# Sixteen-head attentions with the values as stationary blocks: three layers of a twelve-layer kernel rewritten, with new merge lists

## The chip, the cores and the metric

The kernel runs on one core of a Trainium2 chip. The metric is device microseconds of one execution. An execution is one program per engine: TensorE (PE; its weight loads are shown apart as PEld), VectorE (DVE), ScalarE (ACT), GpSimd (POOL), and SyncE (SP), which issues the DMAs. The engines run their own instructions in order and wait for each other on semaphores.

## The reference, cut to what matters

The model is a chain of twelve residual layers over `x` of 64 sequences x 64 tokens x 128 channels, with a context of 128 tokens a sequence. Three of the layers hold a self-attention with 16 heads of 8 channels over the 64 tokens of a sequence; they are what the change touches:

```python
# L1_attn ("lin" in the kernel): linear attention, causal
q, k = relu(q), relu(k)
kv = cumsum(k[..., :, None] * v[..., None, :], axis=2)
num = einsum('bhnd,bhnde->bhne', q, kv)
den = einsum('bhnd,bhnd->bhn', q, cumsum(k, axis=2))[..., None] + 1e-5
y = (num / den) @ wo
# L1_ffn ("m1"): causal softmax attention with rotary positions, then a mixture of experts
attn = softmax(where(causal, q @ k.T / sqrt(8), -inf)); out = (attn @ v) @ wo
# L2_attn ("loc"): softmax attention over the 64 tokens, with biases
o = (softmax(q @ k.T / sqrt(8)) @ v) @ w_out + b_out
```

The other nine are two wide cross-attentions (the costliest layers), a recurrence, a layer of small experts, a single-head cross-attention, a state-space layer, two further mixtures and a sum. They are not changed.

## The kernel before, in words

The 64 sequences are worked off in 4 passes of 2 slots with 8 sequences each. Slot 0 and slot 1 hold independent data (buffers `_0` and `_1`, half of PSUM each, as four banks of 512 float32 columns). Each engine's program for a slot is a generator that stops (`yield`) before each wait. `weave` (L105) merges the two slots' programs on each engine by a list of bits in `ORDER` (L76): the list says, step by step, which slot goes on. So the order on each engine is fixed when the kernel is built, and one slot's work is to fill the other's waits.

All matmuls of the layers concerned are float32. The trace shows each of them as two matmul records (a transpose as one), and the order of the program, quoted below, as one.

A 16-head attention of one slot runs over 4 tiles (`TILES`) of 128 tokens, that is 2 sequences each, after the projections (L617 makes the values, ACT writes them to `Vbd` at L1180):

- the scores of a tile: L800 for "lin", L650 (with the causal mask at L645) for "m1" and "loc";
- DVE masks them (L1655, "lin") or subtracts the maximum (L1627, L1628), and ACT takes the exponential (L1195);
- for softmax, the probabilities are transposed on PE (L677) and copied back by ACT (L1202). "lin" has its scores with the keys on the partitions already;
- `head_outputs` (L628) multiplies them with the values. A block of probabilities, 128 rows (two heads x 64 keys) by 64 queries, is the stationary operand; the values of the two heads, 16 columns, and two columns of ones that give the sums of the probabilities, stream through it: 16 matmuls of 18 columns a tile. The result has the queries on the partitions;
- DVE's `head_out` divides: reciprocal of 16 sums a token (L1614 or L1616; for "lin" an addition of 1e-5 at L1613 first), then a product of 128 columns into `kvT` (L1617).

After the fourth tile `project` transposes the result (four transposes, L471 into bank 1), ACT copies it back to `kvT` (L1115, in "loc" with the bias of the values), and four matmuls with the output weights follow (L486, `ps<-wts,kvT`). There are 3 layers x 4 passes x 2 slots = 24 such attentions, 96 tiles.

PE may start the second half of the transposes of tile t+1 only when `head_out` of tile t is done, since they share a bank; the same holds for the scores of tile t+2 in "lin".

At the program's start the weights that follow a normalisation are centred by one matmul a chunk (L693) with a copy by ACT (L1237), before the first pass goes on.

Of the kernel before, what the change touches and what calls it, by code (L numbers as in the profile page):

```python
# [13 lines left out]
D = 128  # L14
BATCH, SEQ, CTX = 64, 64, 128
SLOTS = 2
GB = 8
# [38 lines left out]
CONSTS = [("ident", 128), ("center", 128), ("hmask8", 8), ("cos", SEQ), ("sin", SEQ),  # L56
          ("causal_add", SEQ), ("causal_T", SEQ), ("upto", 128), ("iota", 16)]


def offsets(table):  # L60
    at, out = 0, {}
    for name, n in table:
# [10 lines left out]
C_AT, C_N = offsets(CONSTS)  # L73


ORDER = dict(  # L76
    pe=(2498, int(""
        "444822181410880258c01020810000335b7b7fb76bb60450b74eddace45a55a981c92142240a7cdd464838a13656dea0b3e9"
        "e32874c2d73bb00200c3ee57fcddffda6c08001268c63565a0105190872de9abc288201348746cb5f6dfebbb0ddc4f3db7fe"
        "ccd9e70cf2bbfffbfaa87448128a095ef7aa13121a19ed291411ded71eaa4d06b72a42000c5edabfcdbeeaefc1446869d553"  # L80
        "948693bfffc288424a0e4805061000d21b9f9db6f5bdbfedc3fae25fe6df4f5cbcc2556baa8351414884057d866e482c288a"
        "cf6b4a37bddf7a377f14856cea20080f17ea7e2ded944a0e00cc745b8884324eddffce42d04622000080026badf7eeeb75f4"
        "85a5b1dde9ffdee5f1e3dad7eff38b448248a058fa73ca13121c38edb4839f4ffffffd67ef77ddffbfff2a38d2db79531010"
        "15fd17f99eaa89608ea7dff", 16)),
    act=(1741, int(""
        "888040194410648209080404e67ff6f67bbef2ab0492a31941100e002110a576bda6f5c23a11356d5141fab51ffffa80826a"
        "8caaee1010b344a904a00b6e14cfbdf67fffbfed30f173477ffe928f0221182100a972fe2903fe58ac4a0b722548fb2d37ff"
        "bb860e7bbe2944555f1901e9c0080840d25793f7dffcbfffefbebb20692a561b012016002084466eedd5f75b6e4b5a0db54a"
        "698f930ffa871a52765b1088acd5b8fe400000201cf6e77becffefbff8cdb35c9d7dd15809026021009a776ce857dffeff7f"
        "79f7b7dbef0c78df748c95e097de0871ff", 16)),  # L90
    dve=(2030, int(""
        "10019c448c84102064c044501430ad2f6ecce5e711071e9739cba21341769d70d150b9b21d1c1e314e2edafd8332312308e7"
        "3466dfaecbbddecf14ca128e5ac0294e48802480148cb6ae89820a5edb6f1f4cfd94675f18f967fff8f03d7e1c3996e71f32"
        "0b8918eb4630d7e30ea3181192b62ccfebb36e6cb77ffdd60d98e25c9022acc6484a45220000086cdddddddccfa5efe4e5f0"
        "f3ac6254b8176f26c4950b89c3d1a0f1453b8ddbd99d672f86641d4fb46e6798b7545f7d87131b30988a175cd5404a204008"
        "183012eddcd9978c8f6a6bff3e78d3b5fd78f137594c655dc2f320b8a196b6b11edefffdf2ffcd7bfff7f1e31c596dbf000e"
        "b27dfd", 16)),
    pool=(610, int(""
        "84c56482d685653532821a33934b77e63fb25c04a2531b1afc0ff65229612d4362fbbb1f8db49519a8887db362b52a42162b"
        "936abfef29e2d841784938a97a33fa9512c28e49fffeb67fd1d", 16)),  # L100
    sp=(26, int(""
        "e0e573", 16)))


def weave(program, order):  # L105
# [5 lines left out]
    for k in range(count - 1, -1, -1):  # L111
# [12 lines left out]
TURNS = ["lat", "rnn", "lora", "lora.c", "x1", "lin", "lin.y", "m1", "m1.y", "rms", "x2.c0", "x2.c1", "x2",  # L124
         "loc", "loc.y", "m2", "m2.oh", "m2.x", "ctx0", "ctx1", "x3", "ssm", "m3", "m3.oh"]
# [30 lines left out]
def build(nc, x, ctxin, ctok_in, fold, cols, weights, consts, out):  # L156
# [4 lines left out]
    with stack:  # L161
# [7 lines left out]
        cst = sb("cst", C_N)  # L169
# [16 lines left out]
        def C(name):  # L186
            at, n = C_AT[name]
            return cst[:, at:at + n]
# [194 lines left out]
        def pair_at(t, bb, j):  # L383
            return 1024 * (t % 2) + 512 * (j // 4) + 256 * bb + 64 * (j % 4)
# [7 lines left out]
        with nc.Block() as block:  # L392
# [71 lines left out]
            def _(pe):  # L464
# [1694 lines left out]
```

## Time and profile before

| | us |
|---|---|
| median of 3 runs (2421.55 to 2429.14) | 2424.98 |
| the profiled execution | 2427.39 |
| its span, first to last instruction | 2425.6 |

TensorE has 2312.0 us of busy time, 95% of the span; VectorE 61%, ScalarE 48%, GpSimd 38%. The mean granted TensorE clock is 0.991 of full speed. The DMA engines are almost idle after the start. A busy PE is not PE at its peak: the end of each matmul is modelled, with the time in which its last results drain.

### The profile page before, as it was taken

To read this page: it belongs to the slowest core of one execution; us is meant where nothing else is said; L and a number is where in the kernel's file an instruction comes from. 1 tells how busy PE (TensorE), PEld (TensorE's weight loads), DVE (VectorE), ACT (ScalarE), POOL (GpSimd) and SP (SyncE) were. 2 spreads that over 40 slices of the span, in tenths; PEclk is the share of its full clock that TensorE was granted. 3 is DMA by queue.
4 is the path that set the end of the run, shared out by engine and by line. 5 is a ranking of instruction groups with operands and counts; after the bars stand their busy time and mean duration, and the time that the engine had idled before them with its cause. 6 is when DMAs were issued, how large, how long until landed. Compare 5 with 4: busy or idle time off the path is not lost.

```text
span 2425.6 us, 41921 instructions
## 1 busy us (share of the span) xinstructions
PE 2312.0 (95%) x16426; PEld 1567.8 (65%) x16426; DVE 1490.3 (61%) x4040; ACT 1163.5 (48%) x2998; POOL 916.8 (38%) x853
## 2 busy tenths in 40 slices
PE   9999989999989999999999999999999999999998
PEld 6766656666766665666666675666666666666665
DVE  6457566666575567666564567756665555665653
ACT  5544334555445533445644453545555445354543
POOL 5334353433234336434332444543323243544310
PEclk9999999999999999999999999999999999999999
DMA  5000000000000000000000000000000000000000
GB/s 235 1 1 1 1 14 1 10 1 27 1 1 1 1 1 10 18 10 1 19 1 1 1 1 5 10 14 10 10 5 1 1 1 1 1 1 1 2 1 14
DMA packets 6821, 26.57 MB, mean 11 GB/s; under 512 B 864, under 2 KB 992, under 8 KB 5984
## 3 DMA queue, kind: packets, MB, share of 16 engines
q1 hardware_dynamic: 6624, 23.89, 2.7%
q8 instruction: 130, 2.13, 0.4%
q14 instruction: 67, 0.55, 0.1%
HBM read 21.79 MB, written 2.10 MB: 10 GB/s over the span
## 4 chain that ended last, share of the span: by engine, by line
PE 75%; DVE 16%; issue 3%; ACT 3%; POOL 3%; DMA 0%; POOLq 0%; DVEq 0%; SPq 0%
PE ps L486 9%; PE ps L499 8%; PE ps L549 7%; PE ps L518 6%; PE ps L510 4%; PE ps L889 4%; PE ps L628 4%; PE ps L603 3%; PE ps L471 3%; PE ps L596 3%; PE ps L650 3%; PE ps L601 3%; PE ps L677 2%; PE ps L846 2%; DVE P L1405 2%
## 5 line engine op out<-in xcount | busy, mean ns | idle before, releaser
L1919 POOL TENSOR_TENSOR P<-P,small 128x384 f32<-128x384 f32 x384 | 316.1, 845 | 564.0 <-DVE small L1430 564.0
L1140 ACT ACTIVATE P<-ps,small 128x192 f32<-128x192 f32 x768 | 315.0, 425 | 134.3 <-DVE small L1422 132.8
L1892 POOL TENSOR_TENSOR small<-small,mhalf 128x4 f32<-128x4 f32 x112 | 126.5, 1130 | 511.9 <-DVE small L1410 255.2
L499 PE MATMUL ps<-kvT,big 128*128 128x192 f32 x1536 | 311.4, 333 | 4.5 <-DVE big L1439 1.8
L499 PEld LDWEIGHTS ps<-kvT,big 128*128 128x128 f32 x1536 | 248.8, 190 | 74.9 <-issue 45.1
L1422 DVE TENSOR_REDUCE small<-ps 128x2 f32<-128x384 f32 x384 | 208.3, 550 | 108.8 <-PE ps L499 100.4
L486 PEld LDWEIGHTS ps<-wts,P 128*128 128x128 f32 x1920 | 232.3, 192 | 45.3 <-issue 30.6
L486 PE MATMUL ps<-wts,P 128*128 128x128 f32 x1920 | 247.8, 278 | 3.8 <-DVE P L1827 2.1
L2009 POOL TENSOR_TENSOR P<-T 128x512 f32<-128x512 f32 x96 | 125.4, 1306 | 197.2 <-DVE T L1709 128.2
L518 PEld LDWEIGHTS ps<-value,big 128*128 128x128 f32 x1536 | 178.6, 192 | 28.3 <-issue 18.6
L518 PE MATMUL ps<-value,big 128*128 128x128 f32 x1536 | 188.0, 278 | 0.1
L549 PE MATMUL ps<-kvT,score 128*128 128x512 f32 x384 | 179.0, 608 | 2.6 <-ACT kvT L1115 2.2
L510 PE MATMUL ps<-cst,P 128*128 128x128 f32 x1152 | 164.8, 275 | 9.0 <-POOL P L1919 3.6
L1140 ACT ACTIVATION_READ_ACCUMULATOR P<-ps,small 128x1 f32 x768 | 160.2, 209 | 0.0
L510 PEld LDWEIGHTS ps<-cst,P 128*128 128x128 f32 x1152 | 131.9, 141 | 32.8 <-issue 12.1
L1315 ACT ACTIVATE P<-ps,col 128x512 f32<-128x512 f32 x128 | 83.3, 685 | 106.8 <-PE ps L893 106.7
L628 PEld LDWEIGHTS ps<-Vbd,P 128*64 128x64 f32 x3072 | 98.8, 138 | 48.2 <-issue 23.9
L549 PEld LDWEIGHTS ps<-kvT,score 128*128 128x128 f32 x384 | 69.7, 192 | 79.5 <-issue 72.5
L1488 DVE SCALAR_TENSOR_TENSOR X<-ps,small,X 128x128 f32<-128x128 f32 x256 | 71.9, 343 | 78.7 <-PE ps L486 75.2
L372 POOL TENSOR_TENSOR big<-big,cst 128x1024 f32<-128x1024 f32 x48 | 103.2, 2155 | 42.7 <-ACT big L1307 23.0
L1627 DVE TENSOR_REDUCE small<-ps 128x8 f32<-128x512 f32 x128 | 87.6, 684 | 50.8 <-PE ps L650 46.9
L1157 ACT ACTIVATE big<-ps 128x512 f32<-128x512 f32 x96 | 57.5, 598 | 122.5 <-PE ps L510 122.4
(287 smaller groups left out, 4495.6 us busy)
## 6 DMA issues: line engine op xcount, KB each, us to landing
ctok<-ctok_dram SPq DMA_DIRECT2D x8, 512.0 KB, 4.1
ctxT<-ctx_dram SPq DMA_DIRECT2D x8, 512.0 KB, 4.1
wts<-weights_dram SPq DMA_DIRECT2D x1, 2530.0 KB, 23.3
wts<-weights_dram SPq DMA_DIRECT2D x1, 2189.0 KB, 17.8
X<-x_dram SPq DMA_DIRECT2D x8, 256.0 KB, 3.5
big<-fold_dram SPq DMA_DIRECT2D x2, 1024.0 KB, 8.5
out_dram<-X SPq DMA_DIRECT2D x8, 256.0 KB, 2.3
wts<-weights_dram SPq DMA_DIRECT2D x1, 1536.0 KB, 25.8
```

The source lines that it names most:

```text
L372: return engine.tensor_tensor(big[s][:, 1024 * (t % 2):1024 * (t % 2) + 1024].rearrange("p (b j t) -> p b j t", b=2, t=SEQ), src[:, 128 * ...
L486: m = pe.matmul(part(s, k, t), tile_of(src, t), w, start=first and t == 0 and c == 0, stop=last and t == TILES - 1 and c == len(pairs) - 1)
L499: m = pe.matmul(ps[s][:, at:at + KEYS], big[s][:, BANK * b + 128 * p:BANK * b + 128 * p + 128], kvT[s][:, keys_at(b):keys_at(b) + KEYS], s ...
L510: m = pe.transpose(part(s, k, p), probs(s, j)[:, PAIR * p + at:PAIR * p + at + 128], C("ident"))
L518: m = pe.matmul(part(s, 1, t), big[s][:, 1024 * t + 128 * k:1024 * t + 128 * k + 128], value[:, at:at + 128], start=(t == 0 and k == 0), s ...
L549: m = pe.matmul(bank(s, qp_bank(g, r) + k), score[:, 128 * block_of(h, nh):128 * block_of(h, nh) + 128], latents(s), start=True, stop=True)
L628: m = pe.matmul(ps[s][64 * bb:64 * bb + 64, at:at + 18], src(bb, j), Vbd[s][:, 18 * (8 * b + j):18 * (8 * b + j) + 18], start=True, stop=True)
L1140: m = act.activation(probs(s, b // 2)[:, to:to + KEYS], ps[s][:, at:at + KEYS], ACT.Exp, bias=small[s][:, 4 * e + p:4 * e + p + 1], accum_ ...
L1422: dve.tensor_reduce(small[s][:, at:at + 2], ps[s][:, BANK * k:BANK * k + 2 * KEYS].rearrange("p (c k) -> p c k", k=KEYS), AX.X, ALU.max, n ...
L1892: pool.tensor_tensor(rstd(s, name, n), variance(s, name, n), mhalf[:, 0:n], ALU.pow).then_inc(*sig("rstd", s))
L1919: m = pool.tensor_tensor(view, view, over(small[s][:, at:at + 2], 2, [128, 2, KEYS]), ALU.mult)
L2009: pool.tensor_tensor(P[s][:, 1024 + 512 * (k % 2):1536 + 512 * (k % 2)], tmp(s, k % 2), tmp(s, 2 + k % 2), ALU.mult)\
```

## The change

The roles in `head_outputs` are swapped. The values are stationary: 128 rows (two heads x 64 keys) by 32 columns of `Vbd`, which is now wider (1536 instead of 1152 columns) and holds 16 value columns and 16 columns of zeros in such a block. The probabilities stream: for each half of the heads, 8 matmuls of 64 columns into four strips of 32 partitions, and 4 matmuls of 128 columns against a block `ones_h`, which give the sums, spread over the 8 channels of each head. That is 16 + 8 matmuls a tile instead of 16. The result comes out with the channels on the partitions. So the four transposes and ACT's copy of `project` are gone. The channels stand in another order, for which the output weights' rows are permuted on the host (`by_head`).

`head_out` now takes a reciprocal of 128 columns instead of 16, and no longer a broadcast.

```diff
 def head_outputs(s, k, t, src, half_ready):
-    for j in range(8):
-        if j % 4 == 0:
-            pe.wait_ge(*half_ready(j // 4))
+    for u in range(2):
+        pe.wait_ge(*half_ready(u))
         for bb in range(2):
-            b, at = 2 * t + bb, BANK * k + 18 * j
-            m = pe.matmul(ps[s][64 * bb:64 * bb + 64, at:at + 18], src(bb, j),
-                          Vbd[s][:, 18 * (8 * b + j):18 * (8 * b + j) + 18], start=True, stop=True)
+            at = BANK * k + 64 * bb
+            for c in range(4):
+                from_ = 16 * u + 48 * (4 * (2 * t + bb) + c)
+                pe.matmul(ps[s][32 * c:32 * c + 32, at:at + 64], Vbd[s][:, from_:from_ + 32], src(c + 4 * u)[:, bb, :],
+                          start=(u + bb == 0), stop=False)
+        at = BANK * k + 128
+        for c in range(4):
+            m = pe.matmul(ps[s][32 * c:32 * c + 32, at:at + 128], ones_h[:, 16 * u:16 * u + 32], src(c + 4 * u),
+                          start=False, stop=(u == 1))
     m.then_inc(*sig("n_o", s))

 def project(s, i, name, w):
     yield
     pe.wait_ge(*on("n_y", s, i, 4 * GROUP[name] + TILES - 1))
-    turn(s, 1, kvT[s])
-    yield
-    pe.wait_ge(*on("zT", s, i, name + ".y"))
     tokens(s, 2, [(kvT[s][:, GT:2 * GT], w)]).then_inc(*sig("y_ps", s))
```

```diff
 # ACT: the values in four activations of 64 x 256 instead of two of 64 x 512
-    m = act.activation(vb[p0:p0 + 64, :, 9 * hh:9 * hh + 8], ...)
+    for u in range(2):
+        m = act.activation(vb[p0:p0 + 64, :, :, 32 * u + 8 * hh:32 * u + 8 * hh + 8], from_[:, u], ACT.Copy)
-def project(s, i, name, bias=0.0):
-    yield from evacuate(s, i, name + ".y", kvT[s][:, GT:2 * GT], bank(s, 1), ACT.Identity, bias=bias)
 # DVE: head_out
-    both = ps[s][:, BANK * k:BANK * k + 9 * NH].rearrange("p (h c) -> p h c", c=9)
+    num, den = ps[s][:, BANK * k:BANK * k + 128], ps[s][:, BANK * k + 128:BANK * k + 256]
+    to, spare = tile_of(kvT[s], TILES + t), tile_of(kvT[s], t)
     if eps:
-        link(dve.tensor_scalar(rec, both[:, :, 8:9], eps, None, ALU.add))
-        link(dve.reciprocal(rec, rec))
+        link(dve.tensor_scalar(spare, den, eps, None, ALU.add))
+        link(dve.reciprocal(spare, spare))
     else:
-        link(dve.reciprocal(rec, both[:, :, 8:9]))
+        link(dve.reciprocal(spare, den))
+    dve.tensor_tensor(to, num, spare, ALU.mult).then_inc(*sig("n_y", s))
```

Three smaller edits go with it. The bias of the values of "loc" is multiplied with the output weights once, at the start: two matmuls and one copy after the centring, for which the first pass waits. Constants that are only used at the start are loaded into a working buffer, by one more DMA, and no longer kept. The matrices `Vbd` and `ones_h` are prepared by other GpSimd memsets.

All merge lists are other ones (here a line of PE's; the numbers tell a reader nothing):

```diff
-    pe=(2498, int(""
-        "444822181410880258c01020810000335b7b7fb76bb60450b74eddace45a55a981c92142240a7cdd464838a13656dea0b3e9"
+    pe=(2475, int(""
+        "1044220b1132b2832008b14b646221010000878dd756ddaf084e3decf77618541e502244101025e1f66402a21227372d51d5"
...
```

What they change is seen in the order of the instructions. Names: `ps_0` and `ps_1` are the slots' PSUM, the numbers behind are columns by the order's own count, and xN counts adjacent equal matmuls. In the changed kernel L491 is what L486 was, L504 L499, L515 L510, L601 L596, L606 to L609 are L601 to L604, L684 is L677, and L634 and L638 are the two kinds of matmul in `head_outputs`.

PE, before, first pass, the last tiles of "lin" in slot 0 and its projection:

```order
L628 MATMUL ps_0<-Vbd_0,P_0 64x18 x32
L510 MATMUL ps_1<-cst,P_1 128x128 x4
L471 MATMUL ps_0<-cst,kvT_0 128x128 x4
L510 MATMUL ps_1<-cst,P_1 128x128 x4
L499 MATMUL ps_1<-kvT_1,big_1 128x192 x2
L486 MATMUL ps_0<-wts,kvT_0 128x128 x4
```

and the same place in the changed kernel:

```order
L634 MATMUL ps_0<-P_0,Vbd_0 32x64 x8
L638 MATMUL ps_0<-P_0,ones_h 32x128 x4
L634 MATMUL ps_0<-P_0,Vbd_0 32x64 x8
L638 MATMUL ps_0<-P_0,ones_h 32x128 x4
L515 MATMUL ps_1<-cst,P_1 128x128 x4
L504 MATMUL ps_1<-kvT_1,big_1 128x192 x2
L601 MATMUL ps_1<-big_1,T_1 128x512
L504 MATMUL ps_1<-kvT_1,big_1 128x192 x2
L491 MATMUL ps_0<-wts,kvT_0 128x128 x4
```

The transposes of slot 0 are gone, and more of slot 1's work stands between the last head outputs and the projection.

PE, before, first pass, the last tile of "m1" in slot 0:

```order
L628 MATMUL ps_0<-Vbd_0,P_0 64x18 x16
L596 MATMUL ps_1<-big_1,T_1 128x512
L471 MATMUL ps_0<-cst,kvT_0 128x128 x4
L601 MATMUL ps_1<-big_1,T_1 128x512
L603 MATMUL ps_1<-Z_1,T_1 128x512
L604 MATMUL ps_1<-Z_1,T_1 128x512
L486 MATMUL ps_0<-wts,kvT_0 128x128 x4
```

and changed, from the tile before the last:

```order
L638 MATMUL ps_0<-P_0,ones_h 32x128 x4
L684 MATMUL ps_0<-cst,P_0 128x128 x8
L634 MATMUL ps_0<-P_0,Vbd_0 32x64 x8
L638 MATMUL ps_0<-P_0,ones_h 32x128 x4
L634 MATMUL ps_0<-P_0,Vbd_0 32x64 x8
L638 MATMUL ps_0<-P_0,ones_h 32x128 x4
L491 MATMUL ps_0<-wts,kvT_0 128x128 x4
L491 MATMUL ps_1<-wts,big_1 128x128 x8
```

Here the projection stands right behind the head outputs, with nothing between them.

## Rows read from the trace of the kernel before

**Rows 1.** The page's busy time by engine, and its chain that ended last.
```profile
PE 2312.0 (95%) x16426; PEld 1567.8 (65%) x16426; DVE 1490.3 (61%) x4040; ACT 1163.5 (48%) x2998; POOL 916.8 (38%) x853
...
PE 75%; DVE 16%; issue 3%; ACT 3%; POOL 3%; DMA 0%; POOLq 0%; DVEq 0%; SPq 0%
```
**Rows 2.** Busy time in two stretches: first "lin", then "m1", of slot 0.
```profile
core 0: us, PE busy (x) PEld busy (x) DVE busy (x) ACT busy (x) POOL busy (x), PEclk, DMA share, GB/s
200.00:215.00 15.00, 14.34 (x206) 11.06 (x204) 11.28 (x35) 4.10 (x15) 6.05 (x7) 1.00 0.01 2
226.00:260.00 34.00, 33.65 (x309) 22.22 (x310) 19.75 (x41) 19.01 (x50) 12.02 (x11) 1.00 0.00 1
```
**Rows 3.** Groups by line: head outputs, transposes, copy and values.
```profile
line engine op names shapes xcount | busy us, mean ns | idle before us <-releasers
L628 PE MATMUL ps<-Vbd,P 128*64 128x18 f32 x3072 | 108.7, 213 | 2.0 <-DVE P L1655 1.1 <-ACT P L1202 0.2
L471 PE MATMUL ps<-cst,kvT 128*128 128x128 f32 x96 | 15.6, 287 | 0.5 <-DVE kvT L1617 0.4
L1115 ACT ACTIVATE kvT<-ps 128x512 f32<-128x512 f32 x16 | 9.6, 597 | 36.7 <-PE ps L471 36.7
L1180 ACT ACTIVATE Vbd<-ps 64x512 f32<-64x512 f32 x48 | 30.3, 631 | 10.9 <-PE ps L617 10.7
L1263 ACT ACTIVATE P<-ps,small 128x128 f32<-128x128 f32 x32 | 11.3, 370 | 10.3 <-DVE small L1593 10.2
```
**Rows 4.** The chain in order of time, start and length in us, around "lin".
```profile
184.84 1.02 PE ps L767 x16
...
194.93 1.08 PE ps L617 x32
...
203.12 1.04 PE ps L628 x32
204.16 0.85 PE ps L499 x4
205.01 0.44 PE ps L510 x4
...
208.83 0.26 DVE small L1614
...
209.12 0.30 DVE kvT L1617
...
209.47 0.66 PE ps L471 x4
210.12 0.44 PE ps L510 x4
210.56 0.65 PE ps L499 x4
211.21 0.90 PE ps L486 x8
```
**Rows 5.** The timeline of PE around a matmul with 32 stationary columns.
```profile
515.16 1.06 PE L982 MATMUL ps<-P,wts 128*32 128x512 f32 x8
516.16 0.65 PE L510 MATMUL ps<-cst,P 128*128 128x128 f32 x4
```
**Rows 6.** Weight loads of 32 and of 64 columns, min/median/max ns.
```profile
L982 PEld LDWEIGHTS ps<-P,wts x64: 106/108/110, 515.2 to 2381.7; 128*32 128x32 f32 x64
L755 PEld LDWEIGHTS ps<-kvT,A x128: 132/137/137, 177.8 to 2084.3; 128*64 128x64 f32 x128
```
**Rows 7.** Groups by line: DVE's reciprocals and products.
```profile
L1430 DVE RECIPROCAL small<-small 128x4 f32<-128x4 f32 x192 | 33.2, 173 | 84.0 <-ACT P L1140 78.4 <-PE ps L628 5.1
L1616 DVE RECIPROCAL small<-ps 128x16 f32<-128x16 f32 x64 | 15.9, 248 | 22.0 <-PE ps L628 21.3 <-DVE P L1399 0.7
L1614 DVE RECIPROCAL small<-small 128x16 f32<-128x16 f32 x32 | 8.1, 253 | 1.1
L1613 DVE TENSOR_SCALAR small<-ps 128x16 f32<-128x16 f32 x32 | 5.3, 165 | 5.2 <-PE ps L628 4.9
L1617 DVE TENSOR_TENSOR kvT<-ps,small 128x128 f32<-128x128 f32 x96 | 28.0, 291 | 3.3
```
**Rows 8.** The chain at the start, after the centring of the weights.
```profile
129.56 0.90 ACT wts L1237 x2
130.46 0.14 issue
130.60 1.95 PE ps L704 x4
```

More of the change, by code:

```diff
@@ L73 @@
 C_AT, C_N = offsets(CONSTS)
+C_KEPT = C_AT["center"][0]
 ORDER = dict(
[L77 to L84 removed]
@@ L123 @@
           "x3.r", "ssm", "m3", "m3.oh", "x0"]
-TURNS = ["lat", "rnn", "lora", "lora.c", "x1", "lin", "lin.y", "m1", "m1.y", "rms", "x2.c0", "x2.c1", "x2",
-         "loc", "loc.y", "m2", "m2.oh", "m2.x", "ctx0", "ctx1", "x3", "ssm", "m3", "m3.oh"]
+TURNS = ["lat", "rnn", "lora", "lora.c", "x1", "lin", "m1", "rms", "x2.c0", "x2.c1", "x2",
+         "loc", "m2", "m2.oh", "m2.x", "ctx0", "ctx1", "x3", "ssm", "m3", "m3.oh"]
 COPIES = [n for n in TURNS if n != "lora.c"]
@@ L187, in C @@
             at, n = C_AT[name]
+            if at >= C_KEPT:
+                return T[1][:, 3 * GT + at - C_KEPT:3 * GT + at - C_KEPT + n]
             return cst[:, at:at + n]
@@ L694, in centre_weights @@
                           .then_inc(center_ps, 1)
+                    yield
+                    n = len(CHUNKS)
+                    pe.wait_ge(centred, n - 2)
+                    to = bank(s, center_bank(n))[:, 0:128]
+                    pe.matmul(to, V("bqkv", 2).to_broadcast([128, 128]), W("loc_o"), start=True, stop=False)
+                    pe.matmul(to, C("ident")[:, 0:1].to_broadcast([128, 128]), W("bo2"), start=False, stop=True).then_inc(center_ps, 1)
                 def rnn(s, i):
@@ L1237, in program @@
                                 act.activation(wts[:, lo:hi], bank(s, center_bank(c))[:, 0:hi - lo], ACT.Copy).then_inc(centred, 1)
+                            yield
+                            act.wait_ge(center_ps, len(CHUNKS) + 1)
+                            act.activation(W("bo2"), bank(s, center_bank(len(CHUNKS)))[:, 0:128], ACT.Copy).then_inc(centred, 1)
                         yield
@@ L1271, in program @@
                         yield from values(s, i, "lin", 2)
-                        yield from project(s, i, "lin")
                         yield from evacuate(s, i, "m1", A[s][:, :], bank(s, 0), ACT.Identity, scale=V("g1"))
@@ L1276, in program @@
                         yield from softmax_heads(s, i, "m1")
-                        yield from project(s, i, "m1")
                         yield from evacuate(s, i, "rms", A[s][:, :], bank(s, 0), ACT.Identity, scale=V("g2"))
@@ L1309, in program @@
                         yield from softmax_heads(s, i, "loc")
-                        yield from project(s, i, "loc", V("bqkv", 2))
                         def hidden(layer, e, func, b1):
@@ L1636, in softmax_heads @@
                             yield from minus_max(t + 2, 0)
-                        yield from head_out(s, i, u0 + t, t, half_bank(t, 0), 0.0)
+                        yield from head_out(s, i, u0 + t, t, half_bank(t, 0))
                         if t < TILES - 2:
@@ L2046, in _ @@
                 pool.memset(ones_b[:, :], 1.0).then_inc(prep, 1)
-                pool.memset(count[:, :], 0.0)
+                pool.memset(count[:, :], 0.0).then_inc(prep, 1)
                 pool.memset(mhalf[:, :], -0.5).then_inc(prep, 1)
                 for s in range(SLOTS):
-                    pool.wait_ge(prep, 3 * s + 2)
                     pool.memset(Vbd[s][:, :], 0.0).then_inc(prep, 1)
-                    pool.wait_ge(prep, 3 * s + 3)
-                    vb = Vbd[s][:, :].rearrange("p (n c) -> p n c", c=18)
-                    pool.memset(vb[0:64, :, 8:9], 1.0).then_inc(prep, 1)
-                    pool.wait_ge(prep, 3 * s + 4)
-                    pool.memset(vb[64:128, :, 17:18], 1.0).then_inc(prep, 1)
+                pool.memset(ones_h[:, :], 0.0).then_inc(prep, 1)
+                pool.wait_ge(prep, SLOTS + 4)
+                for hh in range(2):
+                    for u in range(2):
+                        at = 32 * u + 8 * hh
+                        m = pool.memset(ones_h[64 * hh:64 * hh + 64, at:at + 8], 1.0)
+                    m.then_inc(prep, 1)
                 pool.wait_ge(prep, 3 * SLOTS + 2)
```

95 lines of the change are left out of this document (49 added, 46 removed).

## The prediction

> **What bounds the kernel now.** I read the page's busy time and chain first, then the busy time of two stretches, then the groups by line, the chain in order of time, and single rows for what the change puts in. The page shows PE busy for 95% of the span, and 75% of the chain on PE, 16% on DVE, 3% on ACT [rows 1]. In a stretch with the "m1" attention PE is busy 33.65 of 34 us and DVE 19.75; in "lin" 14.34 of 15, with DVE at 11.28, three quarters [rows 2]. So the kernel is bound by what PE has to stream, and an added DVE microsecond costs something only where PE's next instruction waits for it and the other slot's work has run out. That is nearer in "lin" than in the softmax attentions.
>
> **PE: what goes.** 24 attentions x 4 transposes. Four of them behind other work take 0.44 us (the transposes of L510, the same shape) [rows 4], 24 x 0.44 = 10.5 us; the group's busy time is 15.6 us, with the drain that nothing covered [rows 3]. I take -13.
>
> **PE: what comes.** A tile's head outputs, 16 matmuls, so 32 records of 18 columns, take 1.04 us now [rows 4]. That is not the 18 columns but the loading of 64 stationary columns: L617 has 64 streaming columns with as wide a load and takes 1.08 for 32 records, two strips of the array side by side, so 16 rounds of 0.067. L767, 128 columns in two strips, takes 1.02 for 16 records, 8 rounds of 0.128 [rows 4]. The new block has 32 records of 64 columns and 16 of 128, in four strips. If four strips run abreast, that is 8 x 0.067 + 4 x 0.128 = 1.05 us. Do they? L982 has 32 stationary columns in four strips and 512 streaming ones: 8 records in 1.00 us (515.16 to 516.16) [rows 5]. One after the other they would take 8 x 4 x 0.11 = 3.5 us at the transposes' 0.11 per 128 columns. So they do. The load is shorter too, 108 against 137 ns [rows 6], and the end of the first kind runs into the second, so I take 1.00: 96 x -0.04 = -4 us. What no row shows is how fast short records can follow each other. The densest stretch of the trace is the present block, 32.5 ns a record. At that rate 48 records take 1.56 us, 96 x 0.52 = +50 us. The ends are -5 (rounds as short as their columns) and +50; I take the value near the low end, because L982's rows are the only ones with four strips.
>
> **PE: change of array shape.** Four L499 records take 0.85 us behind the head outputs and 0.65 elsewhere [rows 4]: 0.2 for a change of the tiled shape, and the trace has it before the change as after. I counted the changes of shape in both orders, 737 and 759: 22 x 0.2 = +4.4 us. PE's sum is -13 - 4 + 4.4 = -12.6.
>
> **DVE: the reciprocals.** 4 elements take 173 ns, 16 take 248 [rows 7], 6.3 ns an element; 128 would take 173 + 124 x 6.3 = 950 ns, I take 1.0 us (bounds 0.29, if it ran like the product of 128 columns at L1617, and 1.1). That is 0.75 more, 96 times = 72 us, and 32 additions of 1e-5 over 128 instead of 16 columns, at most 0.29 instead of 0.165 [rows 7], 4 us. DVE goes from 61 to 65% of the span. The Trainium skill, VectorE: DVE Perf Modes, in the walkthrough of the 8-slice pipeline, says that reciprocal is an iterative divide with a repeat count of 8. Worked out as eight passes an element this would be above 1.0 us and add some 10 us of DVE time to the 76, an estimate; the slope of the rows agrees in kind. The sum does not need it.
>
> Behind DVE's reciprocal stand the other slot's maxima and copies, and PE waits for `head_out` at 88 places: the second half of the transposes (48), the scores of tiles 2 and 3 in "lin" (16), the projection (24). From the end of a block to its product DVE needs about 0.65 us now (0.26 + 0.30 and the gaps [rows 4]; 0.85 in "lin") and 1.4 then (1.7 in "lin", or 2.7 where two tiles are queued). I went through both orders and added up, with the durations of rows 4, the other slot's work that stands in between. Before, it falls short by 4 us in total. In the changed order it falls short by 26: 12 at the 64 inner places (five have only four transposes, 0.44 us, in between), 14 at the projections, where three of "m1" have nothing in between. So 22 us more of stalls if each were paid in full.
>
> Against it stands the shorter path. From the transposes' start at 209.47 to the projection at 211.21 [rows 4] are 1.74 us, 0.44 of them PE's own work that is counted above; DVE takes back 0.8. Each attention's result is earlier by 0.5 us, 24 x 0.5 = 12 us if paid in full. Stall and path are of one kind: time of one slot, which counts only as far as the other has nothing to do. I pay both at 0.3, a little over the quarter of the chain that is off PE [rows 1]: 0.3 x (22 - 12) = +3 us.
>
> **The rest.** ACT loses 24 copies of 512 columns at 0.6 to 0.77 and turns 48 activations of 512 columns (631 ns) into 96 of 256; a short one of 128 takes 370 [rows 3], so each about 0.45 and +0.5 us an attention: +13 against -15. ACT is at 48% [rows 1]; nothing. In "lin" the first scores wait for the values, but the new order puts transposes of the other slot there. At the start PE waits for the last centring copy (0.90 and 0.14 us) [rows 8]; two matmuls of 128 columns and a copy of 128 more are +1 us, once. The extra DMA and the memsets lie before that: nothing.
>
> **Sum.** -12.6 + 3 + 1 = -8.6 us. The profiled execution (2427.4, its span 2425.6 and 1.8 around it) becomes 2418.8; it is 2.4 above the median of the runs, so I forecast 2425.0 - 8.6 = 2416.
>
> **Rivals.**
> B: *The short records do not follow each other so fast.* For: nothing in the trace is denser than 32.5 ns a record, and the new block wants 21. Against: L982. Price: in full +50 + 4, 2470; half way 2443. Slower, and it decides from 1.15 us a block. The Trainium skill speaks for it: TensorE: Matmul & The Clock Gate, part 1, states that starts never come closer than about 25 ns however few the columns. By that a block has 48 x 25 = 1.20 us and the sum is +15 or so above mine, an estimate. The rows have 32.5 on average and so don't contradict it.
> C: *DVE stands in front of PE.* The stalls are paid in full and the path gives nothing: -12.6 + 22 + 1 = +10, 2435. For: DVE's three quarters of "lin", the head outputs' DVE rows on the chain there, the places with nothing in between. Against: 58% DVE beside a full PE in "m1".
> D: *The path pays and the order covers the stalls.* -12.6 - 12 + 1 = -24, 2401. For: the planned order puts more of the other slot before the "lin" and "loc" projections. Against: three places with none.
> E: *The change does to PE what it says, but PE's time was not what counted*: the stretches with waits (norms, the recurrence) set the pace, or the new merging gives it back elsewhere. 2425, give or take 5.
>
> **Chances.** Mine 0.40 (own range 2408 to 2425: 0.23 faster, 0.17 the same), B 0.12, C 0.16, D 0.18, E 0.14 (0.11 the same, 0.03 faster). The bound of what a measurement tells from no change is 0.3%, 7.3 us: below 2417.7 is faster, above 2432.3 slower. Faster 0.23 + 0.18 + 0.03 = 0.44; same 0.17 + 0.11 = 0.28; slower 0.12 + 0.16 = 0.28. The range of 8 in 10 goes from 2397, which leaves out a part of D, to 2450, which takes in C and the half of B.
>
> **What the changed profile would show.** The group L471 from `kvT` gone. L634 and L638 together about 1.0 us a tile in the chain; 1.2 or more is B. DVE reciprocals of 128 columns at 0.95 to 1.1 us, DVE's share 64 to 66%; PE's busy time lower by some 10 us. For C: the waits of PE or PEld for DVE `kvT` grow from almost nothing to 20 us or more in total. For D: they stay under 5 and the span is shorter by over 15. I am wrong if the block takes other than 0.9 to 1.15 us, or if the reciprocal is far from 1 us.

## The result and the profile after

The changed kernel takes 2461.6 us (median of four runs, 2461.0 to 2462.9) against 2423.3 us for the kernel before beside it: 1.0153 of its time, 95% interval 1.0138 to 1.0167. It is slower by 37 us by the ratio, 38 by the medians. Forecast were 2416 us, within 2397 to 2450.

Each run below stood beside runs of the kernel before on its own chip, whose median varied from 2423 to 2431 us, so kernels are compared by their ratio to it; 0.001 of it is 2.4 us. The page of the changed kernel, busy times and the chain by engine [rows 1]:

```profile
span 2459.8 us, 44778 instructions
...
PE 2320.9 (94%) x17870; PEld 1541.4 (63%) x17870; DVE 1549.0 (63%) x4040; ACT 1161.5 (47%) x3027; POOL 913.6 (37%) x854
...
PE 76%; DVE 16%; issue 3%; ACT 3%; POOL 2%; DMA 0%; SPq 0%; POOLq 0%; DVEq 0%; ACTq 0%
```

PE has 8.9 us more of busy time where 12.6 us less were expected. The rest of the span, in which PE is not busy, grew from 113.6 to 138.9 us, by 25.3; the two make the 34.2 us between the profiled spans. Nearly all of the 8.9 is the clock: PE was busy for 60 us in stretches at the lower of the two levels (1.2 GHz for 2.4) in the changed kernel, for 43 us before, and half of that is time lost. At full speed its busy time would be 2290.8 us for 2290.5. So the saving on PE isn't there, and the clock took nearly 9 us more. The groups that answer to [rows 3] and [rows 7] (busy us, mean ns of one | idle before, releaser):

```profile
L634 PE MATMUL ps<-P,Vbd 128*32 128x64 f32 x3072 | 81.1, 223 | 3.1 <-DVE P L1662 2.2 <-ACT P L1213 0.2
L638 PE MATMUL ps<-P,ones_h 128*32 128x128 f32 x1536 | 77.6, 274 | 0.0
...
L1624 DVE RECIPROCAL kvT<-ps 128x128 f32<-128x128 f32 x64 | 60.9, 952 | 39.8 <-PE ps L638 39.7
...
L1622 DVE RECIPROCAL kvT<-kvT 128x128 f32<-128x128 f32 x32 | 30.5, 953 | 1.1
```

The busy times of L634 and L638 overlap, so they don't give the length of a block (one tile's head outputs); the chain in order of time does [rows 4]:

```profile
202.79 2.48 DVE P L1662 x4
205.28 0.47 DVE small L1433
205.74 0.21 DVE kvT L1621
205.95 0.02 issue
205.97 0.96 DVE kvT L1622
206.94 0.02 issue
206.96 0.30 DVE kvT L1625
207.26 0.14 issue
207.40 1.09 PE ps L813 x16
208.49 0.36 PE ps L634 x16
208.85 0.22 PE ps L638 x8
209.07 0.22 PE ps L634 x16
209.29 0.22 PE ps L638 x8
```

Two things are to be seen. The block is 0.36 + 0.22 + 0.22 + 0.22 = 1.02 us, which is also the median over the trace. And from 202.79 to 207.26 the chain lies on DVE for 4.5 us: PE's scores of the next tile (L813) wait for the addition (L1621), the reciprocal (L1622) and the product (L1625), and ahead of these stand the masks of "lin" (L1662) and a maximum of the other slot (L1433). PE fills most of it with other work; it stands idle for 0.50 us before L813. PE's waits for a head output (total us, times, longest), in the changed kernel:

```profile
PE ps L491 <- DVE kvT L1625: 11.3, 17, 1.9
PE ps L684 <- DVE kvT L1625: 9.4, 19, 1.7
...
PE ps L813 <- DVE kvT L1625: 2.9, 7, 0.6
```

The same waits in the kernel before:

```profile
PE ps L800 <- DVE kvT L1617: 0.6, 2, 0.3
...
PE ps L471 <- DVE kvT L1617: 0.4, 1, 0.4
...
PE ps L677 <- DVE kvT L1617: 0.2, 1, 0.2
```

L491 is the projection, L684 the second half of the transposes, L813 the scores of "lin": 23.6 us in 43 waits, for 1.2 us in 4.

### The profile page after: what moved, and what is told of

It is laid out like the page before. It is cut to its first block, busy times and chain, and to the rows that moved or that the text cites. A ratio compares the mean times of both kernels' runs of the same rounds, so it can differ in the third digit from the quotient of the medians.

```text
span 2459.8 us, 44778 instructions
## 1 busy us (share of the span) xinstructions
PE 2320.9 (94%) x17870; PEld 1541.4 (63%) x17870; DVE 1549.0 (63%) x4040; ACT 1161.5 (47%) x3027; POOL 913.6 (37%) x854
## 4 chain that ended last, share of the span: by engine, by line
PE 76%; DVE 16%; issue 3%; ACT 3%; POOL 2%; DMA 0%; SPq 0%; POOLq 0%; DVEq 0%; ACTq 0%
PE ps L491 11%; PE ps L504 7%; PE ps L523 7%; PE ps L554 7%; PE ps L515 4%; PE ps L902 4%; PE ps L608 3%; PE ps L859 3%; PE ps L849 3%; PE ps L601 3%; PE ps L606 3%; PE ps L657 3%; PE ps L476 2%; PE ps L684 2%; PE ps L634 1%
## 5 line engine op out<-in xcount | busy, mean ns | idle before, releaser
L504 PE MATMUL ps<-kvT,big 128*128 128x192 f32 x1536 | 310.8, 333 | 10.0 <-ACT P L1153 8.0
L504 PEld LDWEIGHTS ps<-kvT,big 128*128 128x128 f32 x1536 | 248.2, 190 | 85.8 <-issue 55.9
L491 PEld LDWEIGHTS ps<-wts,P 128*128 128x128 f32 x1920 | 236.6, 194 | 50.7 <-issue 38.9
L1433 DVE TENSOR_REDUCE small<-ps 128x2 f32<-128x384 f32 x384 | 207.2, 548 | 85.3 <-PE ps L504 81.8
L491 PE MATMUL ps<-wts,P 128*128 128x128 f32 x1920 | 250.9, 280 | 1.8 <-DVE P L1834 1.4
L515 PE MATMUL ps<-cst,P 128*128 128x128 f32 x1152 | 165.9, 277 | 14.9 <-POOL P L1927 7.6
L515 PEld LDWEIGHTS ps<-cst,P 128*128 128x128 f32 x1152 | 132.3, 142 | 49.3 <-issue 28.2
L1213 ACT ACTIVATE P<-ps 128x512 f32<-128x512 f32 x128 | 74.8, 597 | 87.9 <-PE ps L684 87.6
```

The costliest lines, as they stand in the source:

```text
L491: m = pe.matmul(part(s, k, t), tile_of(src, t), w, start=first and t == 0 and c == 0, stop=last and t == TILES - 1 and c == len(pairs) - 1)
L504: m = pe.matmul(ps[s][:, at:at + KEYS], big[s][:, BANK * b + 128 * p:BANK * b + 128 * p + 128], kvT[s][:, keys_at(b):keys_at(b) + KEYS], s ...
L515: m = pe.transpose(part(s, k, p), probs(s, j)[:, PAIR * p + at:PAIR * p + at + 128], C("ident"))
L1433: dve.tensor_reduce(small[s][:, at:at + 2], ps[s][:, BANK * k:BANK * k + 2 * KEYS].rearrange("p (c k) -> p c k", k=KEYS), AX.X, ALU.max, n ...
```

## The experiments

The change has three parts that can be had apart: the new form (stationary values, no turns), the length of the reciprocal that comes with it, and the new merge lists. "Old order" below is the changed kernel with the merge lists of before. The first theory of the expectations is that the late head output costs, the second that the new lists do. (They give the reciprocal of before as 0.17 us; that is the one of 4 columns, the 16 columns of `head_out` took 0.25.)

**Two by two: the lists and the reciprocal.** The old order keeps empty steps where the removed ones were, and the new last steps of the centring are joined to those before:

```diff
-ORDER = dict( ...lists of the changed kernel... )
+ORDER = dict( ...lists of before... )
 def project(s, i, name, w):
     yield
+    yield
     pe.wait_ge(*on("n_y", s, i, 4 * GROUP[name] + TILES - 1))
```

> The changed kernel's work in the order of before: its own four parts (values as stationary blocks, a sum beside each product, no turns, no copy) are all kept, and only the merge lists of the engines are those of before; where a list still has a step for the removed turn or copy, the step is empty. Theory 1 (latency: a head output now takes VectorE a reciprocal of 0.95 us instead of 0.17, and TensorE's instructions that need the tile come before it is there; no list in use gives them the distance) expects little from the lists: 2440 to 2460 us. Theory 2 (lists: the new lists by themselves place work worse than those of before, over the whole program, and the new head outputs cost what was predicted) expects most of the loss to go: 2415 to 2430 us.

The short reciprocal:

```diff
-link(dve.reciprocal(spare, den))
+link(dve.tensor_scalar(spare, den, 0.01, None, ALU.mult))
```

> The changed kernel with its own lists; in the head outputs the reciprocal of 128 columns (0.95 us) is a multiplication by a constant over the same tile (about 0.28 us), so that the division by the sums is left out. VectorE has 96 x 0.67 = 64 us less to do and each head output is ready 0.67 us sooner. Theory 1 (latency of the head output) expects 2415 to 2430 us. Theory 2 (the lists) expects at most some 10 us back: 2445 us or more.

> Both together: the changed kernel's work in the lists of before, and the cheap multiplication in place of the wide reciprocal (the division by the sums is left out). What stays of the change is the new form of the head outputs on TensorE, without turns and copies. Both theories expect about the predicted -12 us on TensorE and little else: 2405 to 2420 us. A time above 2430 us would say that the new form itself costs, by neither theory.

Measured, as ratio to before with its interval:

| | reciprocal 0.95 us | product in its place |
|---|---|---|
| new lists | 1.0153 [1.0138, 1.0167] | 1.0032 [1.0013, 1.0051] |
| old order | 1.0079 [1.0062, 1.0095] | 0.9982 [0.9971, 0.9993] |

Both theories hold a part, and neither its numbers. The longer reciprocal costs 0.0097 (23.5 us) in the old order and 0.0121 (29 us) in the new; the new lists cost 0.0050 (12 us) with the short operation and 0.0074 (18 us) with the long one. By the intervals the two figures of a pair can't be told apart. What is left of the change without either is -4.4 us.

The product is not as clean a stand-in as planned. From PSUM, in 64 of the 96 tiles, it takes 0.28 us. In "lin" it reads and writes SBUF:

```profile
L1627 DVE TENSOR_SCALAR kvT<-kvT x32: 226/229/1946, 201.9 to 2120.1; 128x128 f32<-128x128 f32 x32
```

Those are the shortest, median and longest in the old order. 17 of the 32 overlapped no GpSimd instruction and took 226 to 229 ns. The other 15 overlapped one, ended some 83 ns behind its end, and took up to 1946 ns: 558 ns in the mean (373 in the new lists). The reciprocal in the same place took 952 to 954 ns each time. So the product gives DVE 53 us back in the old order, not 64, and the runs with half a reciprocal below are the better comparison: against them the full one costs 0.0113 (27 us) in the old order and 0.0154 (37 us, some 7 of them a lower clock) in the new, and the new lists 0.0033 (8 us).

The pages show that the two costs are of different kinds. Old order with the reciprocal, with the product, then the changed kernel's lists with the product:

```profile
PE 2304.0 (94%) x17870; PEld 1537.5 (63%) x17870; DVE 1557.5 (64%) x4040; ACT 1153.2 (47%) x3023; POOL 915.0 (37%) x854
```
```profile
PE 2299.3 (95%) x17870; PEld 1539.0 (64%) x17870; DVE 1504.3 (62%) x4040; ACT 1152.3 (48%) x3023; POOL 916.0 (38%) x854
```
```profile
PE 2311.4 (95%) x17870; PEld 1542.9 (63%) x17870; DVE 1493.0 (61%) x4040; ACT 1160.2 (48%) x3027; POOL 914.0 (38%) x854
```

In all four corners PE has the same 17870 records. Span less PE's busy time is 140.6 (old order) and 138.9 us (new) with the reciprocal, 119.5 (2418.8 - 2299.3) and 120.0 with the product: the reciprocal adds some 20 us of time without PE, and the lists add none. The lists add busy time for the same work, 12.1 and 16.9 us. Most of that is the clock. Core lines of the changed kernel and of the old order:

```profile
core 0: 2459.8 us, clock 0.987
```
```profile
core 0: 2444.6 us, clock 0.992
```

The missing 0.013 of 2459.8 us is 32 us of full-speed time, the missing 0.008 of 2444.6 is 20: 12 us more lost. With the product the profiled clocks are 0.987 and 0.992 again. The traces split each span into three (us); "lost" is half of PE's busy time in stretches at the lower level:

| | PE busy, at full speed | lost to the clock | PE not busy |
|---|---|---|---|
| before | 2290.5 | 21.4 | 113.6 |
| before without turns and copies | 2280.9 | 23.0 | 115.7 |
| old order, product | 2281.1 | 18.2 | 119.5 |
| old order, reciprocal | 2286.4 | 17.6 | 140.6 |
| new lists, product | 2281.8 | 29.6 | 120.0 |
| changed kernel | 2290.8 | 30.1 | 138.9 |

The other executions say the same. One kernel's time moves by about 2 us with each 0.001 of its own clock: the old order with the product took 2418.4 us at 0.994 and 2426.1 at 0.990. The mean clocks over all executions are 0.9850 (new lists) and 0.9919 (old order) with the product, 0.9873 and 0.9932 with the reciprocal, 0.9907 and 0.9935 with half of it. At 2 us for 0.001 that is 14, 12 and 6 us for lists that cost 12, 18 and 8.

Two places of the changed kernel where the clock falls (us, busy time of PE, PEld, DVE, ACT and POOL, granted clock third from the end):

```profile
997.00:1004.00 7.00, 4.06 (x110) 2.95 (x103) 6.26 (x17) 1.19 (x2) 1.08 (x2) 1.00 0.13 27
1004.00:1011.00 7.00, 6.31 (x33) 3.37 (x33) 4.81 (x15) 1.28 (x2) 3.38 (x4) 0.51 0.12 50
2362.00:2369.00 7.00, 3.61 (x18) 1.98 (x16) 6.69 (x29) 1.95 (x4) 1.44 (x1) 1.00 0.00 0
2369.00:2376.00 7.00, 5.13 (x26) 1.18 (x26) 4.91 (x17) 2.60 (x5) 0.00 (x0) 0.53 0.01 2
```

Each time DVE is full (6.26 and 6.69 of 7 us) while PE is busy for little more than half, and in the next stretch PE runs at about half clock. The old order has such places too:

```profile
2380.00:2387.00 7.00, 3.85 (x25) 2.41 (x22) 6.57 (x22) 0.60 (x1) 1.38 (x1) 0.99 0.00 0
2387.00:2390.00 3.00, 3.00 (x16) 2.83 (x15) 1.59 (x8) 0.00 (x0) 1.51 (x4) 0.50 0.02 5
```

Not every fall looks so. Before this one of the changed kernel PE was busy all the time:

```profile
713.00:720.00 7.00, 7.00 (x49) 5.26 (x48) 5.71 (x20) 4.40 (x6) 4.17 (x3) 1.00 0.00 1
720.00:724.00 4.00, 4.00 (x18) 3.40 (x18) 2.65 (x20) 2.74 (x4) 1.27 (x2) 0.59 0.00 0
```

The old order has fewer or shorter ones: 8 stretches at the lower clock, 37 us, against 13 of 65 us. That the lists cost 8 to 18 us is shown by the exchanges; that most of it is lost to the clock is what the traces and the clocks of the executions show, and no run isolates it. Why these lists bring more low stretches stays open. The lists of single engines were not exchanged.

**The same lateness in the kernel before.** One more reciprocal of 88 columns in each head output, nothing else:

```diff
+link(dve.reciprocal(kvT[s][:, GT + 128 * t:GT + 128 * t + 88], ps[s][:, BANK * k:BANK * k + 88]))
 dve.tensor_tensor(kvT[s][:, 128 * t:128 * t + 128]..., ALU.mult).then_inc(*sig("n_y", s))
```

> The kernel before, with nothing else changed, and one more reciprocal in each head output: 88 columns of the same tile into a free place (about 0.7 us), ahead of the last multiplication. 96 x 0.7 = 67 us more for VectorE, and each head output 0.7 us later; lists, turns and copies as before. Theory 1 (latency) expects 20 to 35 us more than before: 2445 to 2460 us. Theory 2 (lists) expects under 10 us more: below 2434 us.

Measured 1.0167 [1.0149, 1.0185], +40 us, above even the first theory's 20 to 35. The reciprocals took 708 ns, and the mean clock was that of the kernel before beside it (0.9908 for 0.9905). The waits for a head output (L471 the projection's transposes, L677 the second half of the transposes, L800 the scores of "lin") that were 1.2 us in the kernel before are now 26:

```profile
PE ps L471 <- DVE kvT L1618: 12.2, 17, 1.8
PE ps L677 <- DVE kvT L1618: 9.9, 20, 0.9
...
PE ps L800 <- DVE kvT L1618: 4.0, 5, 1.0
```

So the loss needs neither the new form nor the new lists.

**Late tile or full queue?** The same reciprocal behind the signal: DVE works as long, the tile is there early. In the new lists with the product (shown), and in the kernel before, where it reads the finished tile and writes a buffer of its own:

```diff
 dve.tensor_tensor(to, num, spare, ALU.mult).then_inc(*sig("n_y", s))
+dve.wait_ge(*on("n_y", s, i, u))
+link(dve.reciprocal(spare[:, 0:88], spare[:, 0:88]))
```

> As the run with the cheap multiplication in place of the wide reciprocal and the changed kernel's own lists (2436 us), with a reciprocal of 88 columns (about 0.71 us) behind the last multiplication of each head output, after its signal: VectorE is busy as in the changed kernel, but the tile is ready early (the division by the sums is left out). If what costs is the time until the tile is there (latency), 2436 to 2445 us. If what costs is VectorE's 64 us more of work, wherever they stand, 2455 to 2462 us.

> The kernel before, nothing left out, with a reciprocal of 88 columns (0.71 us) behind the last multiplication of each head output, after its signal. The same reciprocal ahead of the multiplication cost 39.5 us (2467.8 against 2428.2). Theory 3 (occupancy: what costs is that VectorE's queue, with the other slot's reductions and subtractions behind it, stands 0.7 us longer, and the late tile adds little) expects 30 us or more: 2455 to 2468 us. Theory 1 (latency of the tile) expects under 12 us: below 2437 us.

Measured 1.0145 [1.0117, 1.0173], which is as slow as the changed kernel, and 1.0104 [1.0080, 1.0129], +25 us where the same instruction in front cost 40. Each has, beside the reciprocal's 0.70 us, one more wait of DVE for its own result, so the two places don't differ in the tile's lateness alone. In the kernel before the head outputs stay nearly in time (4.9 us of waits):

```profile
PE ps L472 <- DVE kvT L1618: 3.5, 7, 1.5
...
PE ps L801 <- DVE kvT L1618: 1.2, 3, 0.6
...
PE ps L678 <- DVE kvT L1618: 0.2, 1, 0.2
```

Among the waits that grew are those of the scores for a bank that DVE's subtraction has to free, 1.3 us in the kernel before and 6.9 here:

```profile
PE ps L646 <- DVE P L1631: 4.4, 7, 0.9
...
PE ps L651 <- DVE P L1631: 2.5, 4, 0.9
```

So 25 of the 40 us come with hardly a late tile: behind the reciprocal stand the other slot's maxima and subtractions. Laid beside the kernel before, step by step, PE falls behind most at transposes (8 us) and at the scores of "m1" and "loc" (9 us). The first theory was too narrow. Both ways cost, and they overlap. In the new lists the late reciprocal costs 27 us over the product alone, 25 by the medians. The profiled execution ran at 0.981, but over all executions the mean clock is 0.985 with and without it, so this is not the clock. The waits for a head output are 10.0 us there, for 6.5 with the product alone and 23.6 in the changed kernel: in the new lists, too, most of the cost comes without late tiles.

**Can the order be mended?** In the old order, the two traces with the same order (long and short operation) give for each of PE's steps how much later it starts. Where a step was over 0.3 us late, the other slot's next step was put in front. In these traces L686 is the second half of the transposes, L814 the scores of "lin", L477 and L516 other transposes, and L1630 the product of a head output:

```diff
 PE list, 29 places (17.1 us of lateness)
-... transposes t, second half (slot 0) | attention step (slot 1) ...
+... attention step (slot 1) | transposes t, second half (slot 0) ...
```

> The changed kernel's work in the lists of before (2445 us) with 29 swaps in TensorE's list: wherever the traces of that kernel and of the one with the cheap multiplication in the same order show that a transpose, score or projection step started over 0.3 us late through the reciprocal, the other slot's next step is now in front of it (17.1 us of such lateness in all). Nothing is left out. If that lateness is what the reciprocal costs and cover mends it, half or more of it comes back: 2430 to 2438 us. If cover can't be had without moving the wait elsewhere, 2443 us or more.

> The changed kernel with its own lists and 29 swaps of neighbouring steps in TensorE's list, chosen in the same way from its trace and that of the one with the cheap multiplication (15.2 us of lateness in all, 9.5 us of it in 16 projection steps). Nothing is left out. If cover mends it: 2446 to 2455 us. If the swaps only move the wait: 2458 us or more. The time at half clock (65 us in this kernel's trace, 37 us in the old lists) should stay if it is a matter of the lists as a whole, and fall towards 40 us if it came of these waits.

Measured 1.0118 [1.0097, 1.0139] for the old order, by the ratios 9 us worse than without the swaps, and 1.0246 [1.0229, 1.0263] for the changed kernel's own lists, 23 us worse. The old order's waits before the swaps:

```profile
PE ps L477 <- DVE P L1419: 39.2, 34, 3.0
PE ps L686 <- DVE kvT L1630: 10.0, 20, 0.9
...
PE ps L516 <- POOL P L1932: 5.8, 10, 1.4
```

and after them:

```profile
PE ps L477 <- DVE P L1419: 41.0, 35, 3.0
...
PE ps L516 <- POOL P L1932: 8.4, 11, 2.2
...
PE ps L686 <- DVE kvT L1630: 1.6, 3, 0.7
```

The wait at L686 went from 10.0 to 1.6 us as intended, and came back at steps that had waited less: PE's time without work is 141.3 us for 140.6. By the medians as they stand (2449.5 for 2445.1) the old order lost 4 us, not 9, and the mean clock of 0.991 for 0.993 is as much. So these swaps gained nothing; that they harm by themselves isn't shown. In the other lists the waits for a head output fell too, from 23.6 to 10.0 us, but the time without PE rose from 138.9 to 155.9 us (2479.7 - 2323.8), with a mean clock of 0.985 for 0.987. That the step moved back was itself on its slot's path is the likely reason; no run shows it.

The counterpart on DVE, 27 swaps in its list that let the other slot's maximum or small reciprocal go before a head output:

> The changed kernel's work in the lists of before (2445 us), nothing left out, with 27 swaps of neighbours in VectorE's list: where a head output is followed at once by the other slot's maximum of scores (0.55 us) or reciprocal of sums (0.17 us), that short step now comes first. Theory 3 (the wide reciprocal costs because it stands in front of others) expects some of the 20 us back: 2435 to 2441 us. Theory 1 (the tile is late) expects it worse by what the tiles are later, 2446 to 2455 us. If both weigh the same, or the short steps' inputs aren't there earlier, 2441 to 2447 us.

Measured 1.0093 [1.0071, 1.0116] against 1.0079; the intervals overlap, so not better, and by the ratios 3 us worse. The head outputs are later:

```profile
PE ps L686 <- DVE kvT L1630: 15.2, 21, 1.6
...
PE ps L814 <- DVE kvT L1630: 8.4, 9, 1.7
```

L686 was 10.0 and L814 5.1. So what a place in the queue gave one slot it took from the other, here at least.

**How the cost grows with the length.** Old order, with reciprocals over a part of the 128 columns:

```diff
-link(dve.reciprocal(spare, den))
+link(dve.reciprocal(spare[:, 0:64], den[:, 0:64]))
```

> The changed kernel's work in the lists of before, with the reciprocal over 64 of the 128 columns only (about 0.55 us for 0.95; half of the divisors are left out, so those values are not the reference's). With 0.95 us this order takes 2445 us, with 0.28 us 2424.5 us. If each 0.1 us of it counts alike: 2432 to 2434 us. If there is a slack that the first part of it uses up for nothing: 2424 to 2429 us. If a part of it costs as much as the whole: 2440 us or more.

> The changed kernel's work in the lists of before with reciprocals of 96 of the 128 columns (about 0.75 us; a quarter of the divisors is left out). With 0.28 us this order takes 0.998 of before, with 0.55 us 0.997, with 0.95 us 1.008. If the order has a slack of some 0.3 us that is used up at about 0.55 us and each 0.1 us beyond costs alike: 1.002 (2429 us against 2425). If the slack reaches further: 0.997 to 0.999. If the loss sets in at once: 1.006 or more.

> The same with 112 of the 128 columns (about 0.85 us; an eighth of the divisors is left out). On the line from 0.55 us to 0.95 us it stands at 1.005. A time as that of the full reciprocal or above would say that the cost isn't smooth, and that a few us of any of these comparisons are the luck of one order.

> The changed kernel with its own lists and reciprocals of 64 of the 128 columns (0.55 us; half of the divisors are left out). With 0.28 us these lists take 1.003 of before, with 0.95 us 1.015. If they have the slack of the old lists: 1.001 to 1.004, and the half clock time stays at about 65 us. If they have less cover, as the count of instructions between a head output and what needs it says (26 us short against 4): 1.007 to 1.010.

Waits are PE's for a head output, from the groups of waits; "rest" is span less PE's busy time; the durations are means of each trace; the clock is that of the profiled execution, and behind it the mean over all.

| columns, us | ratio to before | waits | rest | clock |
|---|---|---|---|---|
| product, 0.28 (in "lin" 0.56) | 0.9982 [0.9971, 0.9993] | 5.5 | 119.5 | 0.992, 0.9919 |
| 64, 0.55 | 0.9966 [0.9954, 0.9978] | 4.1 | 120.6 | 0.993, 0.9935 |
| 96, 0.75 | 1.0003 [0.9993, 1.0014] | 9.4 | 131.5 | 0.995, 0.9951 |
| 112, 0.85 | 1.0074 [1.0057, 1.0091] | 12.8 | 135.1 | 0.989, 0.9895 |
| 128, 0.95 | 1.0079 [1.0062, 1.0095] | 15.8 | 140.6 | 0.992, 0.9932 |
| 64, new lists | 0.9999 [0.9990, 1.0009] | 7.9 | 120.2 | 0.989, 0.9907 |

Up to 0.55 us nothing is lost; from there to 0.95 the rest grows by 20.0 us, and 96 x 0.40 = 38 us of DVE's time were added: half of each further microsecond is time without PE, and by the ratios 27 us, seven tenths, are paid. The rest grows fairly evenly, by 3.6 to 5.5 us for each 0.1 us. The time doesn't, because the clock falls in: from 96 to 112 columns the mean clock goes from 0.9951 to 0.9895, at 2 us for 0.001 some 11 us, and the ratio by 0.0071, 17 us. From 112 to 128 columns it rises again, and the ratio hardly moves. Waits at L686, with 64 columns, with 112:

```profile
PE ps L686 <- DVE kvT L1630: 1.4, 5, 0.5
```
```profile
PE ps L686 <- DVE kvT L1630: 7.8, 19, 0.8
```

The new lists with 64 columns lose no time either (rest 120.2): they had the same slack, against the expectation that counted less cover in them; their 0.9999 for 0.9966 goes with a mean clock of 0.9907 for 0.9935. They are even faster than the new lists with the shorter product (1.0032), whose mean clock was 0.9850. The old order with half a reciprocal has the lowest ratio of all, 8 us below the kernel before. But its mean clock was 0.9935 and that of the kernel before beside it 0.9894, which at 2 us for 0.001 is the whole 8 us, and it leaves half of the divisors out. A complete one would have to share the reciprocal with another engine or need fewer columns; that wasn't tried.

**What the removed work was worth.** The kernel before without turns and copies:

```diff
-turn(s, 1, kvT[s])
 yield
-pe.wait_ge(*on("zT", s, i, name + ".y"))
-tokens(s, 2, [(kvT[s][:, GT:2 * GT], w)])
+tokens(s, 2, [(kvT[s][:, 0:GT], w)])
```

> The kernel before without what the change removes: the 24 x 4 transposes of the attentions' results, their wait for ScalarE's copy and the 24 copies (the projections read the result unturned, and the bias of one of them is left out, so those values are not the reference's); the lists are those of before with empty steps in these places. The form of the head outputs, of VectorE's work and of the start are those of before. The prediction's terms for it are 13 us of TensorE and 12 us of a shorter way to the projection, the latter paid at 0.3: -13 to -17 us if those are right, 2409 to 2417 us. The lists theory has no other number. A time of 2420 us or more would say that what was removed had been hidden; under 2405 us that the way to the projection had been paid in full.

The edit also leaves out the copies with their bias. Measured 0.9997 [0.9987, 1.0007]: nothing, where 13 to 17 us were forecast. PE's busy time is 8.1 us shorter, ACT's 13.8, and the rest grew by 2.1:

```profile
PE 2303.9 (95%) x16330; PEld 1559.9 (64%) x16330; DVE 1489.3 (62%) x4040; ACT 1149.7 (48%) x2974; POOL 915.5 (38%) x853
```

The profiled span is 6.0 us shorter, the medians 2. The work is off PE: at full speed 9.6 us, close to the 24 x 0.44 = 10.5 that the prediction's rows give. What gave it back is mostly the clock. The ten executions have a mean of 0.9889, the thirteen of the kernel before beside them 0.9924, and no execution of the one reaches the lowest of the other (0.990 against 0.991). At 2 us for 0.001 that is 7 us. By that estimate the removal is worth some 8 us at an equal clock. Why the clock is lower without the transposes is not shown.

## Why the prediction was wrong, step by step

- *The block on PE* was forecast at 1.00 us and is 1.02. Rival B falls: 16 records of 64 columns take 0.22 us, 14 ns each, and a block of 48 takes 21 ns a record. The Trainium skill, TensorE: Matmul & The Clock Gate, part 1, has starts no closer than about 25 ns, which is 1.20 us a block, an estimate; the trace doesn't agree, and the measurement decides. The prediction put that rule at +15 us above its own sum; 96 x (1.20 - 1.00) is 19.
- *The reciprocal* was forecast at 950 ns by the slope of [rows 7] and took 952; DVE's share went to 63%, near the 64 to 66 named.
- *PE's sum* of -12.6 us of busy time looks right in the old order with the product in place of the reciprocal (2312.0 to 2299.3, -12.7), but that is luck. 3.2 of the 12.7 are a kinder clock. At full speed it is -9.4, and -9.6 for the removal alone: the removal was taken at 13, where 24 x 0.44 = 10.5 would have been near. The new form adds 0.2 us at full speed in the old order, where the block and the change of shape were put at -4 + 4.4 for the new lists. In the old order 6 of the 9.4 came back as time without PE. In the changed kernel PE's busy time is above that of before. That the sum would be paid in full was the hidden assumption; form and removed work together gave -4.4 us of time. Here rival E, which lets the saving be given back elsewhere, was right in part.
- *Stalls and path, both at 0.3.* This is the step that failed. The stalls were costed at 22 x 0.3 and the path was counted against them. They were to cost 6.6 us, the path to give 3.6 back. Measured, the reciprocal in place of the product costs 23.5 us in one order and 29 in the other, and in place of half of itself 27 and 37. No run tells the path's gain from that of the removed work. The count by cover gave 26 us of shortage in the changed order, close to the 23.6 us of named waits; it was the factor that was wrong, and it was taken near the chain's share off PE, a mean over the program, where the places at which PE waits should have been asked. It also counted the late tile alone: DVE's queue behind the reciprocal, which by itself brought 25 us in the kernel before where the reciprocal in front brought 40, had no term.
- *Rival C* (DVE stands in front) had the mechanism of the larger part and its sign in the profile (20 us of waits or more, measured 23.6). Its 2435 us are short of 2461.6 because it still paid the -12.6 in full (8 us too much) and knew no cost of the lists.
- *The merge lists* had no term but cover. They cost 8 to 18 us, and the traces put most of it on the clock, not on waits: 12 us more of full-speed time lost. The clock had no term either.
- *The start* was forecast at +1 us. In the chain of the old order with the product the first pass begins at 130.86 us, where the kernel before has 130.60 [rows 8]: +0.26.

```profile
130.86 1.95 PE ps L718 x4
```

- *ACT's terms* and the one for the change of array shape were not tried apart; PE's busy time has the latter in it.

In sum, from before: -4.4 (form and removal), +23.5 (reciprocal, old order), +18 (lists, with the long reciprocal) = +37. The sum closes by construction; which part gets how much depends on the order of the steps and on the clock of each run.

## What to carry to other kernels

Before an instruction on a second engine is made longer in front of a nearly full TensorE, find the slack at the places that wait for it. Here a reciprocal of 0.55 us cost nothing, and beyond it half or more of every added microsecond was paid, although the engine had a third of its time free. Count the queue behind the longer instruction as well as the result that comes late, and don't book saved TensorE time in full: 9.4 us of it at full speed brought 4.4. Look at the clock of all executions of both kernels before a difference of 10 us is given to the edit. When a short operation stands in for a long one, read its duration in the trace, too. An order found for one set of durations is part of the kernel; single swaps at the places that wait gained nothing in one order and cost some 20 us in the other.

## What was not expected of the hardware

- The granted clock moves with the order as much as with the work. Profiled, the five kernels with the new lists have 0.981 to 0.989, the seven in the old order 0.989 to 0.995, all with the same matmuls. The means over all executions are 0.9850 to 0.9907 and 0.9895 to 0.9951. Within one kernel 0.001 goes with about 2 us.
- Matmuls of 32 stationary columns in four strips start 14 ns apart in the mean of the chain (16 of 64 columns in 0.22 us), where the densest stretch of the kernel before has 32.5 ns a record. In the trace of the changed kernel four strips start 7 ns after each other and the next four 36 ns behind them. Two strips already started 7 ns apart in the kernel before, with 52 ns to the next two.
- DVE's reciprocal grows steadily from 4 to 128 columns: 173, 248, 548, 708 and 952 ns for 4, 16, 64, 88 and 128, or 6.3 ns a column from end to end.
- A short product of DVE from SBUF to SBUF was held up in 15 of 32 cases until a GpSimd instruction ended, for up to 1.7 us; the reciprocal in the same place never was (952 to 954 ns).
